# Graph attention with routing: the rating, the marking and the choice change their places in the order of TensorE and VectorE

## The reference

```python
h = x @ W;  s_src = h @ a[:d];  s_dst = h @ a[d:]
e = s_src[:, :, None] + s_dst[:, None, :]
e = where(e >= 0, e, 0.2 * e);  e = where(A <= 0, -inf, e)
y = softmax(e, -1) @ h                      # x = x + y

logits = layernorm(x) @ Wr + br             # 8 experts
top_p, top_idx = top_k(softmax(logits), 2)
weights = top_p / top_p.sum(-1, keepdims=True)
```

## Time and profile before

| | us |
|---|---|
| median of three runs | 4651.02 |
| profiled execution | 4630.8 |
| its span | 4628.9 |
| TensorE busy (matmuls) | 3536.2 |
| VectorE busy | 2789.2 |
| ScalarE busy | 2067.1 |
| GpSimd busy | 1736.8 |

### The profile page before, as it was taken

The page is one execution under the profiler, slowest core; times in us unless marked ns, Lnnn a source line. Parts: engine busy times, 40 slices in busy tenths (PEclk is TensorE's granted clock), DMA queues, the critical chain, the costliest instruction groups (busy, mean ns, idle before and its releaser), DMA issues. The chain is left out here.

```text
span 4628.9 us, 82058 instructions
## 1 busy us (share of the span) xinstructions
PE 3536.2 (76%) x24355; PEld 2162.1 (47%) x24355; DVE 2789.2 (60%) x10800; ACT 2067.1 (45%) x5218; POOL 1736.8 (38%) x2184
## 2 busy tenths in 40 slices
PE   3999995666666649999987876379847788874994
PEld 1333334444444423333365666357636555542663
DVE  5777756555555566677577767612277576752444
ACT  1777773322222217777632365334347444431221
POOL 3555520000000013433294337744446445434445
PEclk7999995555555559999998987689969999886997
DMA  4444429500000023343100122144342000002445
GB/s 129 125 129 134 127 66 378 245 0 0 0 0 0 0 80 112 116 125 115 54 2 2 35 64 82 37 133 143 119 145 83 1 11 20 15 15 76 131 130 165
DMA packets 235820, 386.93 MB, mean 84 GB/s; under 512 B 25344, under 2 KB 157568, under 8 KB 227136
## 3 DMA queue, kind: packets, MB, share of 16 engines
q1 hardware_dynamic: 217152, 345.83, 23.3%
q0 software_dynamic: 18432, 38.31, 2.4%
HBM read 210.70 MB, written 173.34 MB: 83 GB/s over the span
## 5 line engine op out<-in xcount | busy, mean ns | idle before, releaser
L1482 DVE CUSTOM_DVE_ANT_0 mha_seen<-mha_score,mha_mask 128x512 f32<-128x512 f32 x1024 | 683.3, 688 | 381.6 <-PE mha_score L1245 375.3
L1386 ACT ACTIVATE mha_prob<-mha_turned 128x512 f32<-128x512 f32 x1024 | 587.7, 602 | 308.6 <-PE mha_turned L1259 300.6
L1638 PE MATMUL lstm_gates<-lstm_h_part,lstm_w_part 128*128 128x16 f16 x4608 | 277.2, 179 | 327.9 <-DVE lstm_h_part L1853 324.4
L1245 PE MATMUL mha_score<-mha_k_rows,mha_q_rows 96*128 96x512 bf16 x1024 | 401.1, 394 | 58.9 <-DMA mha_k_rows<-split_rows 38.8
L3192 POOL DMA_INDIRECT expert_rows<-expert_y,expert_target x320 | 307.4, 960 | 367.2 <-DVE expert_y L3338 150.8
L1638 PEld LDWEIGHTS lstm_gates<-lstm_h_part,lstm_w_part 128*128 128x128 f16 x4608 | 215.8, 107 | 481.0 <-DVE lstm_h_part L1853 475.5
L1259 PE MATMUL mha_turned<-mha_q_rows,mha_k_rows 99*128 99x512 bf16 x1024 | 391.3, 383 | 7.6 <-ACT mha_turned L1370 6.5
L1585 POOL TENSOR_TENSOR core_mid<-lstm_hist,lstm_per_unit 128x128 f32 x64 | 29.5, 460 | 886.4 <-DVE lstm_hist L1854 886.4
L1725 ACT ACTIVATE lstm_act<-lstm_gates 128x48 f32<-128x48 f32 x512 | 108.0, 211 | 428.2 <-PE lstm_gates L1638 428.2
L1258 PE MATMUL mha_turned<-mha_maskT,core_ident_bf 128*128 128x512 bf16 x768 | 295.5, 385 | 0.5 <-ACT mha_prob L1386 0.3
L3230 PEld LDWEIGHTS expert_out_ps<-expert_w,expert_hid 128*128 128x128 f32 (+1 forms) x2240 | 262.4, 191 | 38.7 <-issue 35.6
(11 more groups left out here) (558 smaller groups left out, 8854.2 us busy)
## 6 DMA issues: line engine op xcount, KB each, us to landing
routed_rows<-lstm_blank SPq DMA_DIRECT2D x66, 1056.0 KB, 26.9
gat_adj_raw<-adj SPq DMA_DIRECT2D x32, 1024.0 KB, 5.4
mha_q_rows<-split_rows SPq DMA_DIRECT2D x64, 384.0 KB, 4.0
mha_k_rows<-split_rows SPq DMA_DIRECT2D x64, 384.0 KB, 4.9
expert_x<-routed_rows SPq DMA_DIRECT2D x80, 264.0 KB
expert_w<-weights SPq DMA_DIRECT2D x80, 256.0 KB
core_params<-adj SPq DMA_DIRECT2D x16, 1024.0 KB, 5.8
combine_pair<-expert_rows SPq DMA_DIRECT2D x32, 512.0 KB, 4.8
```

Source lines behind the costliest of these rows:

```text
L1245: pe.matmul(score[n % 2][:, :], rows[0][s][0:ROWS, h, t * P:(t + 1) * P], rows[1][s][0:ROWS, h, :], start=True, stop=True).then_inc(S["sco ...
L1386: act.activation(prob[:, n % RING, :], turned[n % 3][:, :], ACT.Exp, scale=-1.0).then_inc(S["prob_ready"], 1)
L1482: dve.tensor_tensor_reduce(seen[n % 2][:, :], score[n % 2][:, :], mask[1 - s][:, t, :], 1.0, 3e38, ALU.add, ALU.min, low[g][:, t, j:j + 1] ...
L1638: return pe.matmul(out, w[:, g * P:(g + 1) * P], h_part[:, part, :], start=False, stop=stop, skip_group_check=True)
```

## The change

On TensorE `route_rate(b - 3)` stands ahead of the transposes `back(b, 0)` and `back(b, 1)` instead of behind them. On VectorE `take` and `lower_logits` come directly behind `maximum`; then come two leaks, then `mark_rows` (which was ahead of `take`), then the third leak. `pick` is no longer one call behind `out`: `weigh` stands between the third and the fourth leak, `compare` behind the fourth, and `order_picks` and `set_gates` stay behind `out`. The other engines' programs and all instructions are the same.

```diff
--- before.py
+++ after.py
@@ -2916,11 +2916,11 @@
                 rows_in(b)
                 project(b)
             for b in range(LAST + 1):
+                if route and 0 <= b - 3 < B:
+                    route_rate(b - 3)
                 if b < B:
                     back(b, 0)
                     back(b, 1)
-                if route and 0 <= b - 3 < B:
-                    route_rate(b - 3)
                 if route and 5 <= b and b % 2:
                     route_count((b - 5) // 2)
                 if b < B:
@@ -3088,21 +3088,31 @@
                 if b + 1 < B:
                     masked(b + 1)
                     maximum(b + 1)
-                if route and 5 <= b and b % 2:
-                    router.mark_rows(dve, (b - 5) // 2, t_ps)
+                picks = route and 4 <= b < B + 4 and b % 2 == 0
                 if route and 0 <= b - 3 < B:
                     router.take(dve, b - 3, rate_ps[(b - 3) % 2])
                     if b % 2 == 0:
                         router.lower_logits(dve, b // 2 - 2)
                 if b + 1 < B:
-                    for t in range(T):
-                        leak(b + 1, t)
+                    leak(b + 1, 0)
+                    leak(b + 1, 1)
+                if route and 5 <= b and b % 2:
+                    router.mark_rows(dve, (b - 5) // 2, t_ps)
+                if b + 1 < B:
+                    leak(b + 1, 2)
+                if picks:
+                    router.weigh(dve, b // 2 - 2)
+                if b + 1 < B:
+                    leak(b + 1, 3)
+                if picks:
+                    router.compare(dve)
                 if b + 2 < B:
                     forbid(b + 2)
                 if b < B:
                     out(b)
-                if route and 4 <= b < B + 4 and b % 2 == 0:
-                    router.pick(dve, b // 2 - 2)
+                if picks:
+                    router.order_picks(dve)
+                    router.set_gates(dve)
             if route:
                 router.table(dve)
```

## The result

The kernel after takes 4617.26 us (median of 4 runs, 4613.11 to 4621.58) against 4650.66 us for the kernel before: ratio 0.9928, 95% interval 0.9914 to 0.9942, so 33.4 us (0.72%) faster. Forecast were 15.4 us; the sign was right, and the gain is more than twice as large and outside the range.

A forecast was written before the change was run, and what follows sets the result against it. GpSimd's own work after the sixth marking ends the stage; TensorE's and VectorE's chains pace the iterations. 7.0 + 3.6 + 2.8 + 2.0 = 15.4 us, so 4651.0 - 15.4 = 4635.6 us; range 4627 to 4650.

The forecast's parts named there:

- The pace and its limits: First joined graph attention: end is the sixth marking plus 65.9 us of GpSimd's own work; even iterations are TensorE's, then VectorE's chain.
- I take 1.0, near the low end, because the slow stretch is the more likely to be fixed: TensorE's rating leaves the chain ahead of `values`: 1.0 us in each of seven iterations, 7.0 us, bounds 5.6 and 11.0.
- more than forecast: Rival: rating shortens TensorE's rest, slow stretches get 1 us shorter in each of twelve iterations; 27 us gain, 4624; chance 0.05.
- The slower rival: Longer TensorE rest in odd iterations keeps the clock at its lower level: 18 us slower, 4669 us; chance 0.11.
- Weigh in the wait: 0.71: Weigh goes into VectorE's 2.40 us wait before the fourth leak: 0.71 us in five even iterations, 3.6 us.
- Less collision: VectorE's pick meets less GpSimd work: 0.7 us per choice in iterations 6, 8, 10, 12; 2.8 us, bounds 0 and 6.0.
- Marking behind two leaks ... Cost: none in the middle.: VectorE's marking starts some 1.8 us later; slack on TensorE and GpSimd's 5.38 us of idle time absorb it, no cost.
- Iteration 14: 2.0: Weigh and compare go into out's 4.43 us wait; marking comes 2.38 us earlier, less 0.4 for the take: 2.0 us.
- GpSimd takes over: Rival: GpSimd's work grows 2 us per pair, its idle time goes and it sets the end; 4646 us, chance 0.10.
- Bounds: Summed lower and upper bounds of the listed terms' gain in the changed stage: 11.2 to 22.6 us.

The follow-up runs named there:

- the scatters only held: Kernel before, with GpSimd's scatter that follows a marking also waiting for the third leak of the next graph; ratio 0.9963, 17 us faster.

## Why the prediction was wrong

| parts in the kernel | gain, us (from the ratio) |
|---|---|
| split | 11 |
| marking | 19 |
| rating | 20 |
| marking, split | 18 |
| marking, rating | 27 |
| rating, split | 32 |
| all | 33 |

(Each is uncertain by 6 to 10 us, so 18 and 19 are one number, and so are 32 and 33.) The parts are not terms of a sum: alone they come to 50 us, together to 33. The prediction added them, and its frame failed at both ends, at one by a wait that it didn't see, at the other by the floor under a pair.

Term by term, up to the sixth marking, the forecast stands against the two profiles like this:

| part of the stage | forecast, us | profiles, us |
|---|---|---|
| up to the fourth leak, iterations 3, 4, 6, 8, 10, 12 (rating) | 6.0 | 13.4, about 4 of it late release |
| behind the fourth leak, iterations 4, 6, 8, 10, 12 (weigh, collision) | 6.4 | 11.4 |
| iteration 14 to the sixth marking | 3.0 | 7.4 |
| odd iterations from 5 on | 0 | 1.7 |
| sum | 15.4 | 33.8 |

- *The pace and its limits.* That the end is the sixth marking plus GpSimd's own work was right in kind: 65.0 us from its first scatter to the last, 65.0 before. But of 5.38 us of waiting I took 1.8 for the delay and 2.5 for the shorter pair and so left 1.1; 0.6 is left. (The delay is 2.9 us, not 1.8: the second marking's scatter starts 6.65 us into iteration 7 before and 9.50 after.) A pair of iterations (8 and 9) went from 40.8 to 34.2 us, of which GpSimd is busy 28.58 (fifth of the busy times):

```profile
2790.62:2824.82 34.20, 24.54 (x168) 22.26 (x166) 28.21 (x96) 21.84 (x52) 28.58 (x42) 0.85 0.30 98
```

Sixteen scatters in it, each with 0.30 us of issue, fill 4.8 of the other 5.6 us. That is GpSimd's floor. Some 6 us a pair could be won, and the change with its side effects won nearly all of it.
- *Rating: "I take 1.0, near the low end, because the slow stretch is the more likely to be fixed".* This step failed. In iteration 8 it is worth 1.58, its upper bound, plus 0.4, and in iteration 4 (the rating alone) 3.1 us, because the slow stretch shortens with it: `values` in the earlier trace rows were back at 1.06 us 6.0 us after the restart, now after 3.9. That was the mechanism of the rival "more than forecast", to which I gave 0.05. How much it is depends on the clock of the execution, and at full clock it is nothing. The Trainium skill, "TensorE: Matmul & The Clock Gate", HAM oscillation, warns of gaps that throttle the engine. The trace agrees from its better side, in this one pair of executions: with the gap partly filled the granted clock of iteration 8 is 0.91 instead of 0.83, and of iteration 10 0.90 instead of 0.76. The slower rival did not come in odd iterations (0.78 to 0.80); one even iteration, 12, had 0.68 and took 21.2 us.
- *Weigh in the wait: 0.71.* Right: about 0.8, and 1.39 us of the wait is left.
- *Less collision: "I take 0.7", bounds 0 and 1.51.* The upper bound came in iterations 8 and 10 (1.5), and more in 6 and 12 (1.9 and 2.4), 7.3 us in all against a bound of 6.0 that was read from iteration 8. Not the split brought it, but the phase: without any split it is gone (8.3 us behind the fourth leak), and with the scatters only held it is gone in iterations 8 and 10 (8.3) and there in 6 and 12 (9.7). The Trainium skill, "SBUF — State Buffer", Who interferes with whom, says that a VectorE instruction with two SBUF inputs and a GpSimd one that reads SBUF contend. L2619 at 0.71 us away from the normalisation agrees with it. But I had named the wrong pair: L2805 ends at 2825.09, before L2619 starts. What runs beside it is L2611 (0.87 us, 0.23 after), and beside L2619 runs the second half of the normalisation, L2807 (2825.17 to 2826.21).
- *"Marking behind two leaks ... Cost: none in the middle."* This step failed too: the same move alone in the kernel before gains 19 us. I asked what waits for the mark and found slack, and didn't ask what the scatters do to others when they run. In the full change it is worth nothing, since GpSimd's queue has taken the marking's place.
- *Iteration 14: 2.0.* With the rating's 1.0 the forecast had 3.0 there; it was 7.4 to the sixth marking. Out waited 4.43 us for a "remote" release in the earlier trace rows that I took for the ordinary end of TensorE's last `values`. It was the late release; after, nothing waits there.
- *GpSimd takes over.* Named, with 4646 us as its price because I let it come by growing work. It came by shrinking pairs and capped the gain instead of spoiling it; the sign that I had named for it, no wait before the sixth marking's scatter, is there.
- *Bounds.* 11.2 to 22.6 us held only the terms I had listed. The row `[1.97 <-remote]` in iteration 8 was in the trace of before, between two rows that I used.

What stays open: by what means scatters delay TensorE's completions, and why mostly when a series of eight has run for 5.6 us or more. It is not the adjacency transfer, and not the granted clock as recorded. A kernel with fewer scatters wasn't tried, since later stages read every row that they write.

## What to carry to other kernels

Before pricing a move on an engine with slack, follow the chain's waits back until each is explained; a wait that ends "remote", with the engine that releases it recorded as done, is a price that the sum can't see and that any shift of another engine's transfers can take away or double. Compute the floor of the next engine per period (busy time plus its issue gaps): it says at once how much all edits together can win, and that their gains will not add. To learn whether an engine's timing rather than its work matters, make it wait a little longer on purpose and time that.

## What the hardware showed that was not expected

- A wait more made the kernel 17 us faster; 1 us more per graph on an engine that waits 5 us per pair made it 7 us slower (1 to 13 by the interval).
- TensorE's completions came up to 5.1 us after the first recorded matmul of a group that is recorded as 1.14 us long, its length at full clock, while GpSimd's scatters ran; ScalarE and VectorE waited for them. Every copy of h that is late by over 0.6 us falls 5.6 us or more behind the first scatter of a series of eight.
- One indirect scatter keeps GpSimd 0.96 us, and 0.30 us more of issue lie between two. Nine in the kernel before take 1.38 to 1.86 us, and VectorE's mask (`forbid`, L3035) runs beside each of them: the scatter ends 0.11 to 0.13 or 0.83 to 0.84 us behind the mask. In all profiles 109 of the 112 scatters of 1.38 us or more overlap such a mask. SyncE's next adjacency load is issued as soon as the mask is done (2788.16 us here), so it stands beside the long scatter without being shown as its cause. In the kernel after, GpSimd and VectorE:

```profile
2787.18 1.79 POOL L2490 DMA_INDIRECT routed_rows<-gat_r_rows,core_slot  x1 [0.31 <-issue]
```

```profile
2786.92 1.22 DVE L3035 TENSOR_SCALAR gat_mask<-gat_adj_raw 128x2048 bf16<-128x2048 int32 x1
```
